# Gathers without GpSimd's rests, and empty list slots read from spread table rows, in a four-layer graph network

## The chip, the cores and the metric

The kernel runs on one core of a Trainium2 chip. The metric is the device time of one execution in microseconds. Engines: PE (matrix), ACT (scalar), DVE (vector), POOL (GpSimd) and SP, which only issues transfers here.

## The reference, cut to what matters

Four graph layers update x (8192 rows of 128 features) with one adjacency matrix of 8192 x 8192 floats, in which about 9 entries of a row are not zero (a density of 0.000976562, and the diagonal). Layers 0, 1 and 3 multiply by the matrix. Layer 2, around which the change lies, takes a maximum over gathered rows:

```python
h = jnp.maximum(_layernorm(x, axis=-1), 0.0)          # layer 2
h = jnp.einsum('ni,oi->no', h, W) + b
_, topk_idx = jax.lax.top_k(adj, 32)
x = x + jnp.max(h[topk_idx], axis=1)
```

A row has some 9 positive entries, so its 32 greatest are these and then the first zero columns. The maximum over the first k zero columns is a prefix maximum, which one table row gives.

## The kernel before

The 64 tiles of 128 rows form 16 groups of 4 tiles. Four stages follow each other.

1. **Adjacency pass.** 256 pieces of 128 x 4 x 512 are loaded; PE turns and multiplies them for layer 0 (L655, L667), ACT copies and marks signs, POOL multiplies by column numbers (L498), DVE takes the 8 greatest keys of each row of each piece (L1473). `pick` (from L1257) makes a group's lists from them: for each tile 3 slots for near neighbours and 6 for far ones, one slot for the prefix row, and for what is left over a pool that the 4 tiles of a group share, of 5, 6, 8 or 12 entries (near) and 12, 14, 17 or 22 (far), by the fullest row of the group. "Near" is 2048 columns, whose part of the table is ready early.
2. **Turned pass.** PE multiplies the stored turned matrix for layer 1 in 8 parts (L751). From each part DVE and ACT make 1024 rows of layer 2's table `h_table` in DRAM (`l1_rows`, L1039 stores them). Ahead of the table lie 65 rows: 64 prefix maxima and, as row 64, one of -3.0e38 (stored at L1047). During this pass POOL gathers for 15 near groups and DVE reduces them (`near_group`).
3. **Chunks.** Layer 3's product runs in 16 chunks of 4 tiles: PE multiplies the 8 parts of a chunk (L783, into two sets of PSUM banks in turn) and DVE adds each part into GR (`add_sums`, L1841 and L1843). PE may be one part ahead: part m needs the sums of part m-2. DVE's loop of a chunk has 8 turns; turns 0 to 3 hold `add_sums` and then one tile of the far maxima (`far_tile`: L1680 adds the mask to gathered rows, L1684 reduces, L1689 and L1692 join, L1717 adds to X), turn 4 `stage_list` (the lists of the group two ahead), turns 5 and 6 `far_own_rows` (L1667, L1668) for the next chunk. Of a new X tile ACT and DVE make layer 3's input (`l3_tile`), which PE needs at the chunk's start.
4. **The end of layer 3** and the stores.

**The gathers.** One `indirect_dma_start` (L506) reads 128 table rows of 512 bytes, one per partition ("lane"), by a column of indices that DVE staged. A near group is 16 gathers for the slots and 5 to 12 for the pool; a far group is 24 and 12 to 22. POOL issues them in a fixed order, waits for `idx_staged` at the start of each group and, for the far pool, for `far_pool_free`. At every fifth gather of a group, counted from its first (k = 0, 5, 10, ...), `rest` runs a POOL instruction pair that computes nothing that is used: an addition of 128 x 512 bf16 onto itself (L517) and a fill of 128 x 384 bytes (L518), both behind a wait for the rests before. The late group (group 0's near part, gathered into GR) has no rests. There are 212 rests and 980 gathers.

**Lanes without a neighbour.** In a tile's own slots an empty entry gets the index of the row's prefix row, as slot 0 does (`pick`, at its end). In a pool slot an empty entry gets key = lane, so the 128 lanes read rows 64 to 191 of the table, and a mask hides what they read (L1541).

Of the kernel before, what the change touches and what calls it, by code (L numbers as in the profile page):

```python
# [10 lines left out]
PREFIX = 64  # L11
NEAR = 4
# [6 lines left out]
BURST = 5  # L19
# [56 lines left out]
def build(nc, x, adj, alpha, w0, b0, w1, w2, b2, w3, b3, out):  # L76
# [22 lines left out]
    NKEY = 3  # L99
    KROWS = 2  # L100
# [9 lines left out]
    table = nc.dram_tensor("h_table", (HEAD + N, P), fp32).ap()  # L110
    near_table = table[0:HEAD + NEAR * PIECE, :]
    early_table = table[0:HEAD + LATE * SGW, :]
    table_v = table[HEAD:HEAD + N, :].rearrange("(t p) f -> p t f", p=P)
# [5 lines left out]
    with ctx:  # L119
# [65 lines left out]
        idle_end = sb("idle_end", [P, 384], u8)  # L185
        lane = sb("lane", [P, 1])
# [30 lines left out]
        idle = D[:, 70 * P:72 * P].bitcast(bf16)  # L217
# [145 lines left out]
        rested = sem("rested")  # L363
# [104 lines left out]
        def _(pool):  # L468
# [8 lines left out]
            pool.iota(lane[:, :], [[0, 1]], base=0, channel_multiplier=1,  # L477
# [11 lines left out]
            pool.iota(row_base, [[STRIDE, TPG]], base=-PREFIX, channel_multiplier=0,  # L489
# [18 lines left out]
            def rests(first, last):  # L508
                return len([k for k in range(first, last) if k % BURST == 0])

            RESTS_N, RESTS_F = rests(0, OWN_N + NEAR_POOL), rests(0, OWN_F + FAR_POOL)
            NO_REST = None
# [12 lines left out]

            def pool_gathers(ring, rows, index, n, cuts, done, so_far, held):
                def leaf(count):
                    most = ring.shape[1]
                    for k in range(count):
                        if so_far is not NO_REST and (held + k) % BURST == 0:  # L530
                            rest(so_far, held + k)
                        share = most * (k + 1) // count - most * k // count
                        gather(ring[:, k, :], rows, index[:, k:k + 1], done, 16 * share)
                    if so_far is not NO_REST and rests(held + count, held + most):
                        pool.sem_inc(rested, 2 * rests(held + count, held + most))
# [5 lines left out]
                with pool.Else():  # L541
                    pool_gathers(ring, rows, index, n, cuts[1:], done, so_far, held)

            def near_gathers(q, n, staged, so_far):
# [3 lines left out]
                own_gathers(near_own[par], near_table, idx_own[par], near_gathered[par], so_far)  # L548
                pool_gathers(near_pool[par], near_table, idx_pool[par], n, NEAR_CUTS, near_gathered[par],
                             so_far, OWN_N)  # L550

            def far_gathers(g, n, staged, free, so_far):
# [3 lines left out]
                own_gathers(far_own[par], table, idx_own[par], far_own_gathered[par], so_far)  # L556
                pool.wait_ge(far_pool_free, free)
                pool.sem_inc(carrier["pool"], 1)
                pool_gathers(far_pools[par], table, idx_pool[par], n, FAR_CUTS, far_pool_gathered[par],
                             so_far, OWN_F)  # L560
# [5 lines left out]
            pool.memset(idle, 0).then_inc(rested, 2)  # L566
            with pool.Fori(0, (NG - 2) // 2) as i:
                for k in range(2):
                    n = pool.value_load(CTL[0:1, 0, bass.ds(i * 2 + (k + 1), 1)], min_val=1, max_val=NEAR_POOL)
                    near_gathers(k, n, i * 2 + (k + 1), i * (4 * RESTS_N) + 2 * k * RESTS_N)  # L570
            n = pool.value_load(CTL[0:1, 0, NG - 1:NG], min_val=1, max_val=NEAR_POOL)
            near_gathers(NG - 2, n, NG - 1, 2 * (NG - 2) * RESTS_N)
            NEAR_RESTS = 2 * (NG - 1) * RESTS_N

            for s in range(SGG, LATE):
# [3 lines left out]
            own_gathers(early_own, early_table, idx_own[1], early_own_gathered, NEAR_RESTS)  # L579
            pool.wait_ge(far_pool_free, 1)  # L580
            pool_gathers(early_pool, early_table, idx_pool[1], n, FAR_CUTS, early_pool_gathered,
                         NEAR_RESTS, OWN_F)

# [15 lines left out]
            own_gathers(late_own, table, idx_own[0], late_gathered, NO_REST)  # L599
            pool_gathers(late_pool, table, idx_pool[0], n, NEAR_CUTS, late_gathered, NO_REST, OWN_N)  # L600

            with pool.Fori(0, (NG - 2) // 2) as i:
                for k in range(2):
                    n = pool.value_load(CTL[0:1, 1, bass.ds(i * 2 + (k + 1), 1)], min_val=1, max_val=FAR_POOL)
                    far_gathers(k + 1, n, i * 2 + (NG + k + 2), i * 2 + (k + 2),
                                i * (4 * RESTS_F) + (2 * (k + 1) * RESTS_F + NEAR_RESTS))
            n = pool.value_load(CTL[0:1, 1, NG - 1:NG], min_val=1, max_val=FAR_POOL)
            far_gathers(NG - 1, n, 2 * NG, NG, 2 * (NG - 1) * RESTS_F + NEAR_RESTS)

        @block.tensor  # L610
        def _(pe):
            pe.wait_ge(s_load, LOADS)
            pe.wait_ge(ident_ready, 4)
# [241 lines left out]
        def _(act):  # L855
# [150 lines left out]
            def l1_rows(s):  # L1006
# [33 lines left out]
                if first == 0:  # L1040
# [6 lines left out]
                    nc.scalar.dma_start(table[0:HEAD, :], pfxn[:, :]).then_inc(head_stored, 16)  # L1047
# [131 lines left out]
        def _(dve):  # L1179
# [78 lines left out]
            def pick(g):  # L1258
# [6 lines left out]
                kn = keys[:, near, :, :].rearrange("p c r e -> p (c r e)")  # L1265
                kfar = keys[:, far, :, :].rearrange("p c r e -> p (c r e)")
# [817 lines left out]
```

## Time and profile before

| what | value |
|---|---|
| device time, median of 3 runs (lowest, highest) | 3695.63 us (3692.3, 3698.97) |
| span of the profiled execution | 3738.5 us |
| PE busy | 3378.0 us, 90% |
| DVE busy | 2622.0 us, 70% |
| POOL busy | 2592.6 us, 69% |
| ACT busy | 1607.0 us, 43% |
| gathers to slots in D, to pool slots in D, to pool slots in ATS | 624 of 1007 ns, 215 of 983 ns, 117 of 1002 ns |
| rests: additions, fills | 212 of 1051 ns, 212 of 428 ns |

The profiled execution has no time of its own beside its span; what lies around the span is not shown. The span is 42.9 us above the median of the runs. Busy time is that of an engine's own instructions; an engine that waits, branches or issues counts as idle. A share of the span is a mean over the four stages.

### The profile page before, as it was taken

Reading aid. Unit: us, or ns where it says so; the run is one execution under the profiler, and the core shown is the slowest. Engines: PE = TensorE matmul, PEld = TensorE weight load, DVE = VectorE, ACT = ScalarE, POOL = GpSimd, SP = SyncE. Lnnn points to the kernel's source line nnn. Section 1 sums busy time; section 2 is a strip of 40 time slices with the busy share of each in tenths; the row PEclk is TensorE's granted clock in tenths of the full one; section 3 lists DMA queues with packets and bytes.
Section 4 is the critical chain, followed back from the end, with each engine's and each line's share of the span. In section 5 each row is a group of like instructions: output and inputs, shape, how many; then the busy total and the mean of one; then the engine's idle time right before and its main releaser. Section 6 shows DMA issues by size and latency. Waiting matters only on the chain.

```text
span 3738.5 us, 76487 instructions
## 1 busy us (share of the span) xinstructions
PE 3378.0 (90%) x29444; PEld 3342.4 (89%) x29444; DVE 2622.0 (70%) x5491; ACT 1607.0 (43%) x3554; POOL 2592.6 (69%) x2448
## 2 busy tenths in 40 slices
PE   6999999999999999999999999942899898989894
PEld 6999999999999999999999999942888898989894
DVE  6788888788788788211177664647787878878767
ACT  6777887787787786222122211221111111112114
POOL 3998998998998997000487856647888878777500
PEclk9999999999999999999999999975999999999997
DMA  6999999999999999788888888842788887878781
GB/s 217 397 396 367 388 385 352 386 389 352 386 391 351 384 376 388 276 291 296 290 322 319 299 294 311 293 154 77 269 286 291 300 308 284 295 280 308 259 293 57
DMA packets 401324, 1155.22 MB, mean 309 GB/s; under 512 B 36717, under 2 KB 56110, under 8 KB 401006
## 3 DMA queue, kind: packets, MB, share of 16 engines
q1 hardware_dynamic: 360096, 1082.21, 78.4%
q0 software_dynamic: 31360, 64.29, 5.5%
q10 hardware_dynamic: 9550, 4.69, 0.4%
q8 instruction: 174, 2.85, 0.3%
q14 instruction: 144, 1.18, 0.1%
HBM read 874.19 MB, written 276.86 MB: 308 GB/s over the span
## 4 chain that ended last, share of the span: by engine, by line
PE 65%; DVE 21%; issue 5%; POOL 4%; ACT 2%; DMA 1%; another core or an unknown queue 1%; DVEq 1%; POOLq 0%; SPq 0%; ACTq 0%
PE psU L667 18%; PE psT L751 18%; PE psT L655 9%; PE psT L783 8%; PE psU L751 6%; DVE agg L1684 4%; DVE HT L1680 3%; PE psU L783 3%; DVE D L1473 2%; POOL D L498 2%; POOL D L506 2%; DVE GR L1843 1%; DVE W L1684 1%; DMA adj_turned<-ATS 1%
## 5 line engine op out<-in xcount | busy, mean ns | idle before, releaser
L498 POOL TENSOR_TENSOR D<-D,iota 128x512 f32<-128x512 f32 x1024 | 1307.3, 1307 | 115.9 <-ACT D L910 97.6
L667 PE MATMUL psU<-HB,ATS 128*128 128x129 f32 x8192 | 1007.1, 276 | 28.4 <-ACT ATS L903 26.3
L667 PEld LDWEIGHTS psU<-HB,ATS 128*128 128x128 f32 x8192 | 961.1, 193 | 33.3 <-ACT ATS L903 28.6
L783 PE MATMUL psT<-ATS,PIECES 128*128 128x129 f32 x6144 | 804.7, 281 | 172.7 <-ACT ATS L1069 79.3
L783 PEld LDWEIGHTS psT<-ATS,PIECES 128*128 128x128 f32 x6144 | 751.5, 196 | 186.3 <-issue 143.8
L1473 DVE MAX8 D<-D 128x8 f32<-128x512 f32 x1024 | 644.2, 683 | 259.7 <-POOL D L498 251.9
L751 PE MATMUL psT<-GR,PIECES 128*128 128x129 f32 x6144 | 780.7, 276 | 20.1 <-issue 19.3
L751 PEld LDWEIGHTS psT<-GR,PIECES 128*128 128x128 f32 x6144 | 733.2, 192 | 24.9 <-issue 24.2
L506 POOL DMA_INDIRECT D<-h_table,idx_own x624 | 628.4, 1007 | 170.4 <-issue 150.3
L903 ACT ACTIVATE ATS<-psT 128x512 f32<-128x512 f32 x1024 | 555.9, 596 | 270.4 <-PE psT L655 177.1
L910 ACT ACTIVATE D<-PIECES 128x1024 f32<-128x1024 f32 x512 | 544.1, 1063 | 0.0
L655 PE MATMUL psT<-ident,PIECES 128*128 128x128 f32 x4096 | 530.7, 273 | 0.0
L655 PEld LDWEIGHTS psT<-ident,PIECES 128*128 128x128 f32 x4096 | 465.1, 142 | 0.1
L751 PE MATMUL psU<-GR,PIECES 128*128 128x129 f32 x2048 | 317.3, 276 | 11.3 <-issue 11.2
L783 PE MATMUL psU<-ATS,PIECES 128*128 128x129 f32 x2048 | 320.3, 279 | 3.2 <-issue 3.0
L517 POOL TENSOR_TENSOR D<-D 128x512 bf16<-128x512 bf16 x212 | 222.8, 1051 | 117.4 <-DVEq L60 103.2
L751 PEld LDWEIGHTS psU<-GR,PIECES 128*128 128x128 f32 x2048 | 272.0, 192 | 14.5 <-issue 14.4
L783 PEld LDWEIGHTS psU<-ATS,PIECES 128*128 128x128 f32 x2048 | 276.4, 196 | 4.9 <-issue 4.8
L1053 ACT ACTIVATE junk_rows<-X 128x128 f32<-128x128 f32 x64 | 19.8, 309 | 569.0 <-DVE X L1717 334.8
L506 POOL DMA_INDIRECT D<-h_table,idx_pool x215 | 211.2, 983 | 71.8 <-issue 53.3
L1843 DVE TENSOR_TENSOR GR<-psT,GR 128x387 f32<-128x387 f32 x240 | 122.5, 552 | 138.0 <-PE psU L783 102.3
L1684 DVE TENSOR_REDUCE agg<-HT 128x128 f32<-128x896 f32 (+2 forms) x120 | 187.4, 1562 | 4.1
(410 smaller groups left out, 2896.9 us busy)
## 6 DMA issues: line engine op xcount, KB each, us to landing
PIECES<-adj_turned SPq DMA_DIRECT2D x512, 1024.0 KB
PIECES<-in_adj SPq DMA_DIRECT2D x256, 1024.0 KB
adj_turned<-ATS SPq DMA_DIRECT2D x512, 512.0 KB, 8.2
D<-h_table,idx_own POOLq DMA_INDIRECT x624
h_table<-HB ACTq DMA_DIRECT2D x8, 512.0 KB, 6.6
D<-h_table,idx_pool POOLq DMA_INDIRECT x215
out_x<-X SPq DMA_DIRECT2D x3, 1024.0 KB, 5.1
ATS<-h_table,idx_pool POOLq DMA_INDIRECT x117
```

Source lines behind the costliest of these rows:

```text
L498: pool.tensor_tensor(key, key, iota[:, :], ALU.mult).then_inc(keyed, 1)
L506: pool.indirect_dma_start(slot, None, rows, bass.IndirectOffsetOnAxis(ap=index, axis=0)).then_inc(done, inc)
L517: pool.tensor_tensor(idle, idle, idle, ALU.add).then_inc(rested, 1)
L655: last = nc.tensor.transpose(psT[h][:, b * GROUP + r * P:b * GROUP + (r + 1) * P], pieces[n % SLOTS][:, r, x0:x0 + P], ident[:, :])
L667: last = nc.tensor.matmul(sum4(r), AT[K % NAT][:, b * GROUP + r * P:b * GROUP + (r + 1) * P], HB[:, j, :], start=(j == 0 and r % 2 == 0), ...
L751: last = nc.tensor.matmul(acc(s % 2, r), block_of(q % SLOTS, b, r), GR[:, j, :], start=(j == 0 and opens(r)), stop=(j == NT - 1 and closes ...
L783: last = nc.tensor.matmul(acc(h, r), block_of(slot, b, r), Hc[par][:, jj, :], start=(jj == 0 and opens(r)), stop=(jj == CT - 1 and closes(r)))
L903: nc.scalar.activation(AT[K % NAT][:, half], psT[K % 2][:, half], ACT.Copy).then_inc(pair_copied, 1)
L910: nc.scalar.activation(KEY[n % NKEY][:, rows, :], pieces[n % SLOTS][:, rows, :], ACT.Sign)\
L1473: last = v.max(cand[g % 2][:, c, r, :], KEY[n % NKEY][:, r, :])
L1684: v.tensor_reduce(part_max[k], kept[:, 0:size, :].rearrange("p k f -> p f k"), AX.X, ALU.max)\
L1843: last = v.tensor_tensor(sums, acc_rows(m % 2, n), sums, ALU.add)
```

## The change

Three things are changed.

- **Rests.** `rest`, its counter `rested`, its tiles and all 212 calls are gone. Waits for `idx_staged` and `far_pool_free` stay.
- **Empty own slots.** `pick` has two more DVE instructions for each group: where a list of 8 keys has an empty entry, it gets the list's first (greatest) key, so that the lane reads its first neighbour's row once more. A list with no key at all still reads the prefix row.
- **Table head and pools.** The 65 head rows are stored 16 times (1040 rows, 532 KB in place of 33 KB), and each 8 lanes use a copy of their own. An empty pool entry has key = 15 x lane (near) or 47 x lane (far), so that lanes read rows spread over the table. DVE has 18 more small instructions before the adjacency pass, to work out each lane's copy.

```diff
+COPIES = 16
-BURST = 5
...
+    NEAR_STEP, FAR_STEP = 15, 47
...
+    BASE = COPIES * HEAD
+    table = nc.dram_tensor("h_table", (BASE + N, P), fp32).ap()
+    heads_v = table[0:BASE, :].rearrange("(c p) f -> p c f", p=HEAD)
...
-            pool.iota(lane[:, :], [[0, 1]], base=0, channel_multiplier=1,
+            pool.iota(lane[:, 0:1], [[0, 1]], base=0, channel_multiplier=NEAR_STEP,
+                      allow_small_or_imprecise_dtypes=True).then_inc(ident_ready, 1)
+            pool.iota(lane[:, 1:2], [[0, 1]], base=0, channel_multiplier=FAR_STEP,
...
-            def rest(so_far, held):
-                pool.wait_ge(rested, so_far + (2 * rests(0, held) + 2))
-                pool.sem_inc(carrier["pool"], 1)
-                pool.tensor_tensor(idle, idle, idle, ALU.add).then_inc(rested, 1)
-                pool.memset(idle_end[:, :], 0).then_inc(rested, 1)
-
-            def own_gathers(ring, rows, index, done, so_far):
+            def own_gathers(ring, rows, index, done):
                 for k in range(ring.shape[1]):
-                    if so_far is not NO_REST and k % BURST == 0:
-                        rest(so_far, k)
                     gather(ring[:, k, :], rows, index[:, k:k + 1], done, 16)
...
-                        if so_far is not NO_REST and (held + k) % BURST == 0:
-                            rest(so_far, held + k)
...
-                    nc.scalar.dma_start(table[0:HEAD, :], pfxn[:, :]).then_inc(head_stored, 16)
+                    nc.scalar.dma_start(heads_v, pfxn[:, :].unsqueeze(1).to_broadcast([HEAD, COPIES, P])).then_inc(head_stored, 16)
...
+                lists, fills = [a.rearrange("p r (l k) -> p (r l) k", k=8) for a in (top, topd)]
...
+                pk.mark(v.scalar_tensor_tensor(fills, lists, 0.0, lists[:, :, 0:1].to_broadcast([P, 2 * TPG, 8]),
+                                               ALU.is_equal, ALU.mult))
...
+                pk.mark(v.tensor_tensor(lists, lists, fills, ALU.add))
...
-                pk.mark(v.tensor_copy(IDXN[:, ts, 0], sp[:, 3, :]))
+                pk.mark(v.tensor_scalar(IDXN[:, ts, 0], sp[:, 3, :], lane[:, 2:3], None, ALU.add))
...
-                link(v.scalar_tensor_tensor(key, empty, lane[:, 0:1], key, ALU.mult, ALU.add))
+                link(v.scalar_tensor_tensor(key, empty, lane[:, 0:1] if near_list else lane[:, 1:2], key, ALU.mult, ALU.add))
...
+            link(v.memset(lane[:, 2:3], 0.0))
+            for k in range(1, COPIES):
+                link(v.scalar_tensor_tensor(lane[:, 2:3], lane[:, 0:1], float(NEAR_STEP * k * (P // COPIES)) - 0.5,
+                                            lane[:, 2:3], ALU.is_gt, ALU.add))
+            link(v.tensor_scalar(lane[:, 2:3], lane[:, 2:3], float(HEAD), None, ALU.mult))
+            link(v.tensor_scalar(row_base, row_base, lane[:, 2:3], None, ALU.add))
```

POOL's order of instructions in a near group, as it was: the last gather to slots (idx_own), with the rest ahead of it, and the pool's gathers (idx_pool) in the case of 5 entries. Ahead of these rows stand three times a rest and five gathers to slots.

```order
L515 REGISTER_ALU
L517 TENSOR_TENSOR D<-D 128x512
L518 MEMSET idle_end 128x384
L506 DMA D<-h_table,idx_own 128x128
L539 COMPARE_AND_BRANCH
L506 DMA D<-h_table,idx_pool 128x128 x4
L515 REGISTER_ALU
L517 TENSOR_TENSOR D<-D 128x512
L518 MEMSET idle_end 128x384
L506 DMA D<-h_table,idx_pool 128x128
```

The whole near group of 21 gathers, as it is now:

```order
L508 DMA D<-h_table,idx_own 128x128 x16
L523 COMPARE_AND_BRANCH
L508 DMA D<-h_table,idx_pool 128x128 x5
```

The four rests of the slots and the one in the pool are gone, and 21 gathers follow each other; nothing else moved. A far group loses eight to ten rests in the same way.

DVE before the adjacency pass, now:

```order
L1860 TENSOR_SCALAR alph<-alph 128x1
L1862 MEMSET lane 128x1
L1864 SCALAR_TENSOR_TENSOR lane<-lane 128x1 x15
L1866 TENSOR_SCALAR lane<-lane 128x1
L1867 TENSOR_SCALAR D<-D,lane 128x4
L1868 COPY psY<-D 128x64
L1869 COPY psY<-own 128x4
```

Of these rows the 18 instructions on `lane` and `row_base` stand between the one on `alph` and the two copies, which were neighbours.

## Rows read from the trace of the kernel before

**Rows 1.** The page: the span, and busy time of each engine.

```profile
span 3738.5 us, 76487 instructions
...
PE 3378.0 (90%) x29444; PEld 3342.4 (89%) x29444; DVE 2622.0 (70%) x5491; ACT 1607.0 (43%) x3554; POOL 2592.6 (69%) x2448
```

**Rows 2.** Chunks: us, busy us (instructions) by engine, PEclk, DMA share, GB/s.

```profile
3000.00:3300.00 300.00, 277.71 (x2366) 273.52 (x2365) 242.51 (x381) 44.99 (x184) 242.12 (x264) 0.97 0.83 298
```

**Rows 3.** PE's waits, 2700 to 3540: us in total, times, longest.

```profile
PE psT L783 <- DVE GR L1843: 52.1, 24, 5.4
PE psT L783 <- issue: 25.9, 37, 3.0
```

**Rows 4.** DVE's and POOL's waits, 2700 to 3540.

```profile
DVE GR L1843 <- PE psU L783: 68.8, 17, 7.0
...
DVE HT L1680 <- issue: 13.6, 15, 1.7
...
POOL D L517 <- DVEq L60: 28.5, 4, 8.3
```

**Rows 5.** POOL in order of time: start, us, what [idle before].

```profile
2835.12 0.94 POOL L506 DMA_INDIRECT D<-h_table,idx_own  x1 [0.30 <-issue]
2836.37 0.94 POOL L506 DMA_INDIRECT D<-h_table,idx_own  x1 [0.30 <-issue]
2837.32 1.06 POOL L517 TENSOR_TENSOR D<-D 128x512 bf16<-128x512 bf16 x1
...
2838.90 0.98 POOL L506 DMA_INDIRECT D<-h_table,idx_own  x1 [0.17 <-POOL idle_end L518]
```

**Rows 6.** DVE in order of time.

```profile
2822.14 1.75 DVE L1680 TENSOR_TENSOR HT<-D,iota 128x768 f32<-128x768 f32 x1
```

**Rows 7.** DVE's groups with rests, 2597 to 3523: busy us, mean ns.

```profile
L1680 DVE TENSOR_TENSOR HT<-D,iota 128x768 f32<-128x768 f32 x32 | 36.2, 1131 | 1.9 <-DVE GR L1849 0.9
...
L1680 DVE TENSOR_TENSOR HT<-ATS,iota 128x768 f32<-128x768 f32 x24 | 28.7, 1194 | 2.7 <-issue 1.3 <-DVE GR L1849 0.9
...
L1689 DVE TENSOR_TENSOR agg<-agg 128x128 f32<-128x128 f32 x55 | 22.3, 405 | 1.9
```

**Rows 8.** The same after the last rest, 3524 to 3600.

```profile
L1680 DVE TENSOR_TENSOR HT<-ATS,iota 128x768 f32<-128x768 f32 x8 | 7.6, 955 | 1.0 <-DVE GR L1849 0.9
...
L1689 DVE TENSOR_TENSOR agg<-agg 128x128 f32<-128x128 f32 x5 | 1.5, 292 | 0.2
```

**Rows 9.** DVE at the start of the chunks, in order of time.

```profile
2579.90 1.61 DVE L1623 TENSOR_TENSOR HB<-HB,agg 128x128 f32<-128x128 f32 x1
...
2620.89 1.09 DVE L1680 TENSOR_TENSOR HT<-ATS,iota 128x896 f32<-128x896 f32 x1 [10.48 <-issue]
```

**Rows 10.** PE at the start of the chunks, in order of time.

```profile
2630.25 2.95 PE L783 MATMUL psT<-ATS,PIECES 128*128 128x129 f32 x12 [8.33 <-DVE GR L1841]
...
2697.90 2.47 PE L783 MATMUL psT<-ATS,PIECES 128*128 128x129 f32 x12 [3.82 <-issue]
```

**Rows 11.** PE's waits in the turned pass with gathers, 1820 to 2460.

```profile
PE psT L751 <- issue: 18.2, 30, 1.1
PE psU L751 <- issue: 11.2, 21, 1.0
```

**Rows 12.** Stretches around two rests (columns of Rows 2).

```profile
2011.50:2013.00 1.50, 1.50 (x16) 1.50 (x15) 0.00 (x0) 1.37 (x8) 1.44 (x3) 1.00 1.01 407
...
2042.80:2044.30 1.50, 0.91 (x9) 0.89 (x9) 1.47 (x2) 0.00 (x0) 1.41 (x3) 1.00 0.87 333
```

**Rows 13.** Queues, 2700 to 3540: packets, MB, share of 16 engines.

```profile
q1 hardware_dynamic: 54316, 209.43, 68.4%
q0 software_dynamic: 16049, 32.89, 12.3%
```

**Rows 14.** DVE waiting in the adjacency pass: in total, and the first time.

```profile
DVE D L1473 <- POOL D L498: 251.9, 202, 3.9
...
63.36 1.29 DVE L1473 MAX8 D<-D 128x8 f32<-128x512 f32 x2 [3.87 <-POOL D L498]
```

More of the change, by code:

```diff
@@ L506, in gather, with pool_gathers @@
                 pool.indirect_dma_start(slot, None, rows, bass.IndirectOffsetOnAxis(ap=index, axis=0)).then_inc(done, inc)
[L508 to L512, printed above, removed]
-            def rest(so_far, held):
-                pool.wait_ge(rested, so_far + (2 * rests(0, held) + 2))
-                pool.sem_inc(carrier["pool"], 1)
-                pool.tensor_tensor(idle, idle, idle, ALU.add).then_inc(rested, 1)
-                pool.memset(idle_end[:, :], 0).then_inc(rested, 1)
-            def own_gathers(ring, rows, index, done, so_far):
+            def own_gathers(ring, rows, index, done):
                 for k in range(ring.shape[1]):
-                    if so_far is not NO_REST and k % BURST == 0:
-                        rest(so_far, k)
                     gather(ring[:, k, :], rows, index[:, k:k + 1], done, 16)
-            def pool_gathers(ring, rows, index, n, cuts, done, so_far, held):
+            def pool_gathers(ring, rows, index, n, cuts, done):
                 def leaf(count):
@@ L541, in pool_gathers, with near_gathers @@
                 with pool.Else():
-                    pool_gathers(ring, rows, index, n, cuts[1:], done, so_far, held)
-            def near_gathers(q, n, staged, so_far):
+                    pool_gathers(ring, rows, index, n, cuts[1:], done)
+            def near_gathers(q, n, staged):
                 par = q % 2
@@ L598, in _ @@
             pool.wait_ge(idx_staged, NG + 1)
[L599 to L600 removed]
+            own_gathers(late_own, table, idx_own[0], late_gathered)
+            pool_gathers(late_pool, table, idx_pool[0], n, NEAR_CUTS, late_gathered)
             with pool.Fori(0, (NG - 2) // 2) as i:
@@ L1353, in pick @@
                 for into, (_, to, count) in zip((IDXN[:, ts, 1:], IDXF[:, ts, :]), parts):
-                    pk.mark(v.tensor_tensor(into, topd[:, :, to:to + count],
-                                            sp[:, 3, :].unsqueeze(2).to_broadcast([P, TPG, count]), ALU.add))
+                    pk.mark(v.scalar_tensor_tensor(into, topd[:, :, to:to + count], lane[:, 2:3],
+                                                   sp[:, 3, :].unsqueeze(2).to_broadcast([P, TPG, count]),
+                                                   ALU.add, ALU.add))
                 pk.settle()
@@ L1544, in stage_list @@
                 link(v.scalar_tensor_tensor(at_row, o3, -float(STRIDE), at_row, ALU.mult, ALU.add))
-                mark(v.tensor_scalar(idx_pool[par][:, 0:count], at_row, float(PREFIX), None, ALU.add))
+                mark(v.tensor_scalar(idx_pool[par][:, 0:count], at_row, float(BASE - 1), None, ALU.add))
                 mark(v.tensor_scalar(keep[par][:, 0, 0:count], keep[par][:, 0, 0:count], NOT_HERE, None, ALU.mult))
```

50 lines of the change are left out of this document (19 added, 31 removed).

## The prediction

> **What bounds the kernel now.** I read the page first: the span is 3738.5 us and PE is busy for 90% of it [rows 1]. A share is a mean over stages, so I then read the waits of PE in each stage that has gathers; the adjacency pass has none, and nothing there waits for them. In the turned pass PE waits for no other engine to speak of: from 1820 to 2460 it stands still 18.2 + 11.2 = 29.4 us in 51 short pauses of 1.1 us at most that the trace gives no releaser for [rows 11]. PE is the bound of that stage, so these pauses count in full. In the chunks PE works 277.7 of 300 us, DVE 242.5 and POOL 242.1 [rows 2], and POOL's figure leaves out 0.30 us of issue behind each gather [rows 5], so POOL hardly rests there either. Who waits for whom tells more: PE waits 52.1 us for DVE's sums and 25.9 us more without a releaser [rows 3], pauses up to 3.0 us long that fall on the same turns; DVE waits 68.8 us for PE but only 13.6 us, 15 times, before the first mask addition of a group; POOL waits 28.5 us for DVE [rows 4]. So the bound of the chunks is PE, held up in turns 0 to 3 by DVE's far tiles, and not the gathers. Only at the stage's start is it the gathers: DVE stands 10.48 us before the first far tile [rows 9], and PE then 8.33 us and, a chunk later, 3.82 us [rows 10].
>
> **The rests, POOL's own time.** Two gathers start 1.25 us apart, and 2.53 us with a rest between them [rows 5]: a rest takes 1.28 us of POOL. 212 of them are 271 us, nearly all where nobody waits for POOL. The exception is the start. Group 1 has 8 rests, 8 x 1.28 = 10.2 us, before its last gather, and DVE's wait is 10.48 us [rows 9]: it goes almost whole. Of PE's 8.33 + 3.82 = 12.2 us behind it [rows 10] I take **12 us**. What is late next is DVE itself, which had finished its other work 10.5 us before; from then on POOL's start on a group is set by DVE's `stage_list`, so the rest of POOL's time turns into longer waits for DVE.
>
> **The rests, DVE's stalls.** A mask addition of 128 x 768 takes up to 1.75 us where a rest runs beside it [rows 6], and 955 ns after the last rest [rows 8]. Over the chunks the mean with rests is 1131 ns of 32 and 1194 ns of 24 [rows 7]: (1131 - 955) x 32 + (1194 - 955) x 24 = 5.6 + 5.7 = 11.4 us for this one shape. L1689 stalls by (405 - 292) x 55 = 6.2 us [rows 7, 8]. The shape 128 x 896 (56 of them) I take at half a stall of these, 0.12 us each: 7 us. With some 9 us for the others (L1692, L1717, L1849, other widths), an estimate at the same share, about 33 us of stall fall in turns 0 to 3. Where DVE sets the pace of these turns PE gets this back one for one, where PE does, nothing: bounds 0 and 33, and since two thirds of the groups have lists of 14 entries or more and show PE waiting, I take **23 us**. Before the chunks' start a stalled L1623 takes 1.61 us [rows 9] and 292 ns unstalled by the nearest like instruction [rows 8]; four of them are on the path to the first chunk, **4 us**. The clock: PEclk is 0.97 from 3000 to 3300 [rows 2]; PE waits stand ahead of what is lost. Of some 900 us the missing 3% is 27 us, and for the waits that go I take a fifth of it, **5 us**.
>
> **The rests, PE's pauses.** Rows 12 show a rest after five gathers and one after two: 1.5 us hold 9 matmuls in the one and 16 in the other. A rest alone therefore costs PE nothing; five gathers and a rest do. The pauses are 29.4 us in the turned pass [rows 11] and in the chunks I take half of the 25.9 us [rows 3], 12 us, since the longer ones of up to 3.0 us look like waits for DVE. What ends when the rests go is open: all 41 us (the rest is needed for a pause), nothing, or it gets worse (below). The span is also 42.9 us longer than the median run, close to this sum, so the recorded execution may have pauses that others lack. I take a third, **14 us**, and keep 0 and 41 as ends. [...]
>
> **The spread rows.** The gathers' queue moved 32.89 MB for 12.3% of the DMA engines, the loads' 209.43 MB for 68.4% [rows 13]: 0.374 against 0.327 % per MB. If spreading made gathered rows as cheap as loads, 32.89 x 0.047 = 1.6% of DMA time would be free; if it cost as much more, the 80.7% in use would be 82.3%. PE waits for no load that a row shows, so either way I count 0. DVE's two instructions for each group (32 in all, under 0.5 us each by the small groups' durations: at most 16 us) lie in the adjacency pass, where DVE waits 251.9 us for POOL [rows 14]; its 18 instructions before that pass, at about 0.2 us each 3.6 us, fit in the 3.87 us for which it waits first [rows 14]. The larger head store (0.5 MB once, ACT's queue) is half a store of a table part, eight of which are hidden. All 0; if the cover were gone, 4 us.
>
> **The sum.** 12 + 23 + 4 + 5 = 44 us, and 14 us of pauses: 58. The profiled span would be 3738.5 - 44 - 41 = 3654 us if all pauses went. The median run: 3695.6 - 58 = 3638, rounded to **3640 us**.
>
> **Rivals.**
> - *The burst, slower.* PE's pause begins with the backlog of some four gathers and the rest only ends it. For it: after two gathers there is none [rows 12], and the 5 may mark where it begins. Against: most of a pause lies within the rest itself. Then, with no rest, PE would go on at 9 in place of 16 matmuls per 1.5 us, 44% lost, until POOL stands still. If each of 15 near groups lost 44% of 12 us and each of 15 far groups 44% of 20 us, that is 79 + 132 = 211 us, less the 44: 3695.6 + 167 = 3863 us. It decides from about 3 us of such slow work per group (44 / 0.44 / 30). Milder forms lie between 3700 and 3770.
> - *PE has it anyway.* The denser gathers (one per 1.25 us, 52 KB/us in place of 43) hold up loads, whose engines are in use for 83% [rows 2], and DVE's time saved is lost to waits for PE (68.8 us now, rows 4). Then only the start's 16 us remain: 3680 us.
> - *The change does not do what it says.* If many lanes on one row were no cost (0.374 against 0.327 allows it), the spread is without effect and the rests decide alone: the forecast stands, or the first rival. It has no chance of its own.
> - *All pauses go, in every run*: 3695.6 - 44 - 41 = 3611 us.
>
> **How the numbers follow.** Forecast 0.44; all pauses go 0.14; PE has it anyway 0.15, of which a third within 0.2%; the burst 0.27, of which 0.02 ends within 0.2%. A measurement of this kernel tells about 0.2% (7 us) from no change. Faster: 0.44 + 0.14 + 0.10 = 0.68. Same: 0.05 + 0.02 = 0.07. Slower: 0.25. The range takes in the forecast with its bounds, 3611 less 16 for stalls that all count, and of the burst what is milder than 3770: 3595 to 3770 us. About 0.17 lies above it, next to nothing below.
>
> **What would show it.** POOL's gathers 1.25 us apart through a group; mask additions of 128 x 768 near 955 ns throughout; no 10 us wait of DVE at the start of the chunks; PE's waits for L1843's counterpart down by a third; longer idle times of POOL. Wrong: PE with more and longer pauses inside groups of gathers than 51 and 1.1 us in the turned pass, or PE waiting for loads.

## The result: 26% slower, and the profile after

The change takes 4658.0 us (median of 4 runs, 4654.2 to 4662.1), the kernel before on the same chip 3697.3 us. The ratio is 1.2609, 95% interval 1.2592 to 1.2627. Forecast were 3640 us and a range up to 3770; the sign belongs to the first rival, which gave 3863 us. In the profiled execution the span is 4652.5 us where it was 3738.5 [rows 1], 914 us more. By the timed runs it is 961 us: the trace of the kernel before is 41 us longer than its timed runs on this chip, and as long as those on three other chips below (3737 to 3742 us). One run of the first experiment below took 5209.99 us at a granted clock of 0.629; it stays unexplained and is left out of that experiment's ratio.

The page of the change: the span, busy time, and the slices of PE, of its granted clock and of the DMA engines (tenths, 40 slices).

```profile
span 4652.5 us, 75668 instructions
...
PE 3568.3 (77%) x29444; PEld 3479.4 (75%) x29444; DVE 2532.9 (54%) x5541; ACT 1609.7 (35%) x3554; POOL 2247.9 (48%) x2024
...
PE   6999999999999998576685781366666565666695
...
PEclk9999999999999999787897885677777777777897
DMA  6999999999999887465675662355555554555673
```

PE has the same 29444 matmuls and is busy for 190 us more: its clock is granted at 0.861 of full speed on average, where it was 0.963, and a matmul that stands alone shows as 0.38 us where in a full row one is done every 0.11 us (65 in 7.00 us, below). The other 724 us are idle time of PE. No other engine is loaded more: DVE and POOL fell [rows 1], the DMA engines moved 248 GB/s over the span where it was 309, and ACT is where it was. The stretches say where (us, busy us and instructions of PE, PEld, DVE, ACT, POOL, then PEclk, DMA share, GB/s):

```profile
0.00:1480.00 1480.00, 1415.73 (x12562) 1408.21 (x12563) 1191.11 (x2632) 1141.95 (x1963) 1304.49 (x1037) 0.99 0.97 367
1480.00:1800.00 320.00, 318.90 (x2854) 318.55 (x2853) 84.40 (x330) 85.06 (x292) 8.08 (x8) 1.00 0.84 294
1800.00:2300.00 500.00, 344.24 (x2684) 332.06 (x2682) 178.80 (x451) 71.88 (x232) 184.21 (x192) 0.80 0.60 200
...
3300.00:3800.00 500.00, 331.41 (x2527) 316.07 (x2527) 241.31 (x437) 54.02 (x220) 161.03 (x171) 0.79 0.56 188
```

The adjacency pass and the first part of the turned pass are as before to within 1% of PE's matmuls (12562 and 2854 in the first two stretches, 12651 and 2866 before). The loss starts within 10 us of the first gather, which comes at 1823.8 us. From 1800 to 2300 PE does 2684 matmuls; in the kernel before it did 4158 in the same stretch, with a clock of 1.00. PE's waits from 1500 to 4600 (total, times, longest):

```profile
PE psT L761 <- issue: 429.0, 252, 74.4
PE psT L729 <- issue: 209.5, 164, 3.1
PE psU L761 <- issue: 163.2, 94, 3.8
PE psU L729 <- issue: 73.6, 55, 2.4
PE psT L761 <- DVE GR L1826: 48.8, 24, 4.7
```

875 us in 565 pauses have no releaser by these four rows. One of them, of 74.4 us, is no new loss: it is PE's wait between the layers, which the kernel before has too. First the row of the change, then that of the kernel before:

```profile
2924.13 2.94 PE L761 MATMUL psT<-ATS,PIECES 128*128 128x129 f32 x12 [74.42 <-issue]
```

```profile
2597.80 2.94 PE L783 MATMUL psT<-ATS,PIECES 128*128 128x129 f32 x12 [79.28 <-ACT ATS L1069]
```

That leaves 801 us, where the two stretches of [rows 3, 11] had 25.9 and 29.4 us. The wait for DVE's sums (L1826, before L1843) is what it was. No row has PE waiting for a load from 1500 to 4600, while SP waits with its loads (L439) 797.8 + 472.7 us for matmuls of PE, and 1190.9 us for what the trace does not name, from 1800 to 4600. One run of gathers shows the pattern, the 38 gathers from 3040.9 on (columns as above):

```profile
3041.00:3048.00 7.00, 7.00 (x65) 7.00 (x64) 6.83 (x11) 0.00 (x0) 5.48 (x6) 1.00 0.89 322
3048.00:3088.00 40.00, 9.03 (x36) 6.90 (x35) 1.97 (x3) 0.00 (x0) 30.24 (x33) 0.57 0.29 82
3088.00:3097.00 9.00, 4.58 (x18) 4.14 (x18) 1.36 (x3) 0.00 (x0) 0.08 (x1) 0.50 0.18 46
3097.00:3102.00 5.00, 5.00 (x43) 5.00 (x42) 0.78 (x2) 0.00 (x0) 0.00 (x0) 0.91 0.92 351
```

For 7 us and 6 gathers PE keeps its 9.3 matmuls per us. Then it does 36 in 40 us, a tenth, until the last gather, and 18 in the 9 us behind it. Then it is back. Seen singly, in another run of gathers (start, us, what [idle before]), first PE and then POOL in the same microseconds:

```profile
1863.36 0.38 PE L729 MATMUL psU<-GR,PIECES 128*128 128x129 f32 x1 [2.42 <-issue]
1866.16 0.38 PE L729 MATMUL psU<-GR,PIECES 128*128 128x129 f32 x1 [2.42 <-issue]
...
1890.66 0.38 PE L729 MATMUL psT<-GR,PIECES 128*128 128x129 f32 x1 [0.32 <-issue]
1891.36 0.38 PE L729 MATMUL psT<-GR,PIECES 128*128 128x129 f32 x1 [0.32 <-issue]
```

```profile
1862.92 0.95 POOL L508 DMA_INDIRECT D<-h_table,idx_own  x1 [0.30 <-issue]
1864.18 0.94 POOL L508 DMA_INDIRECT D<-h_table,idx_own  x1 [0.31 <-issue]
```

One matmul comes every 2.8 us in the middle of a piece, where no semaphore is waited for, and after the last gather one every 0.70 us. PE's granted clock is 1.00 up to 3048 us, and is 0.57 and then 0.50 in the stretches behind it: 1.00 still from 3050 to 3052, when PE already pauses (2 matmuls in 2 us), 0.88 from 3052 to 3054 and 0.50 from there. I call this state of PE **starved**, without saying of what. Of the parts that I had expected, one is plain to see: DVE's mask additions (L1663, before L1680) are at their undisturbed 955 ns of [rows 8], from 3000 on:

```profile
L1663 DVE TENSOR_TENSOR HT<-D,iota 128x768 f32<-128x768 f32 x32 | 30.6, 957 | 1.9 <-DVE GR L1832 0.9
```

### The profile page after: what moved, and what is told of

Same layout as the page of the kernel before. It is cut to its first block, busy times and chain, and to the rows that moved or that the text cites. A ratio compares the mean times of both kernels' runs of the same rounds, so it can differ in the third digit from the quotient of the medians.

```text
span 4652.5 us, 75668 instructions
## 1 busy us (share of the span) xinstructions
PE 3568.3 (77%) x29444; PEld 3479.4 (75%) x29444; DVE 2532.9 (54%) x5541; ACT 1609.7 (35%) x3554; POOL 2247.9 (48%) x2024
## 3 DMA queue, kind: packets, MB, share of 16 engines
q0 software_dynamic: 31360, 64.29, 5.2%
## 4 chain that ended last, share of the span: by engine, by line
PE 63%; issue 19%; DVE 15%; ACT 1%; DMA 1%; DVEq 1%; POOL 0%; SPq 0%; ACTq 0%
PE psU L645 17%; PE psT L729 16%; PE psT L761 11%; PE psT L633 8%; PE psU L729 5%; PE psU L761 4%; DVE agg L1667 3%; DVE HT L1663 2%; DVE GR L1826 1%; DVE D L1456 1%; DVE W L1667 1%; POOL D L500 0%; DVE agg L1672 0%; DMA adj_turned<-ATS 0%; DVE X L1980 0%
## 5 line engine op out<-in xcount | busy, mean ns | idle before, releaser
L508 POOL DMA_INDIRECT D<-h_table,idx_own x624 | 595.2, 954 | 1650.2 <-DVEq L60 1218.0
L761 PE MATMUL psT<-ATS,PIECES 128*128 128x129 f32 x6144 | 888.5, 289 | 481.3 <-issue 429.0
L761 PEld LDWEIGHTS psT<-ATS,PIECES 128*128 128x128 f32 x6144 | 809.3, 204 | 529.1 <-issue 518.5
L729 PE MATMUL psT<-GR,PIECES 128*128 128x129 f32 x6144 | 835.5, 283 | 211.5 <-issue 210.6
L729 PEld LDWEIGHTS psT<-GR,PIECES 128*128 128x128 f32 x6144 | 774.4, 199 | 232.7 <-issue 232.6
L1826 DVE TENSOR_TENSOR GR<-psT,GR 128x387 f32<-128x387 f32 x240 | 122.6, 552 | 681.8 <-remote 553.4
L761 PE MATMUL psU<-ATS,PIECES 128*128 128x129 f32 x2048 | 346.5, 288 | 163.6 <-issue 163.2
L761 PEld LDWEIGHTS psU<-ATS,PIECES 128*128 128x128 f32 x2048 | 294.8, 203 | 167.5 <-issue 167.5
L729 PE MATMUL psU<-GR,PIECES 128*128 128x129 f32 x2048 | 333.0, 283 | 73.7 <-issue 73.6
L729 PEld LDWEIGHTS psU<-GR,PIECES 128*128 128x128 f32 x2048 | 285.6, 199 | 78.2 <-issue 78.2
L1791 DVE TENSOR_TENSOR HB<-psY,bias 128x512 f32<-128x512 f32 x16 | 11.1, 692 | 498.2 <-PE psY L698 498.2
```

Source lines behind the costliest of these rows:

```text
L508: pool.indirect_dma_start(slot, None, rows, bass.IndirectOffsetOnAxis(ap=index, axis=0)).then_inc(done, inc)
L729: last = nc.tensor.matmul(acc(s % 2, r), block_of(q % SLOTS, b, r), GR[:, j, :], start=(j == 0 and opens(r)), stop=(j == NT - 1 and closes ...
L761: last = nc.tensor.matmul(acc(h, r), block_of(slot, b, r), Hc[par][:, jj, :], start=(jj == 0 and opens(r)), stop=(jj == CT - 1 and closes(r)))
L1826: last = v.tensor_tensor(sums, acc_rows(m % 2, n), sums, ALU.add)
```

## Experiments

Eighteen experiments ran on five chips, called A to E in order of time, with runs of the kernel before beside them: 3737.1 us on chip A, 3737.9 on B, 3670.0 on C, 3671.2 on D and 3742.2 on E. These chips turned out to matter, so each result is told with its chip. No chip was used at two times, so what is said of a chip may also belong to its hour. All are edits of the kernel before, unless it is said that they start from the change.

### Chip A: rests or spread rows

The change with `BURST`, `rest` and its two instructions put back, word for word:

> The change with the rests put back: spread rows, and an addition and a fill before every fifth gather as before. Theory A (the missing rests alone make PE slow: it issues one matmul per 2.8 us while gathers follow each other, and the rests ended such spells): back to 3697 us, within 15 us. Theory B (the spread rows do it: lanes without a neighbour read 16 heads and many more places of the table, and that traffic holds up what PE's queue is fed by): it stays above 4300 us, since the rests cover only one gather in five. A mixture would lie between.

Measured: 3745.1 us, ratio 1.0026 (1.0006 to 1.0045). The expected 3697 us was the time of the kernel before on the result's chip; against the 3737.1 us of this one the loss is gone. Its pauses in the turned pass, 1820 to 2460, are those of before and fewer:

```profile
PE psT L757 <- issue: 17.0, 33, 1.0
PE psU L757 <- issue: 6.7, 14, 0.8
```

The counterpart takes only the rests away (`at_rest` also stands in the two conditions ahead of `rest`):

```diff
-            def rests(first, last):
-                return len([k for k in range(first, last) if k % BURST == 0])
+            def at_rest(k):
+                return False
+
+            def rests(first, last):
+                return len([k for k in range(first, last) if at_rest(k)])
```

> The kernel before with nothing taken away but the rests; lanes without a neighbour still read one row. Theory A: as slow as the change, 4658 us within 20. Theory B: no slower than 3700. If the spread had been a help beside the loss (many lanes on one row slow a gather by 50 ns), this one is slower than the change, by up to 30 us.

Measured: 4672.2 us, ratio 1.2508 (1.2471 to 1.2545). Theory A holds from both sides: the missing rests are the whole loss, and the spread rows have no part in it beyond 0.3%. Then the rest in pieces:

```diff
             def rest(so_far, held):
...
-                pool.tensor_tensor(idle, idle, idle, ALU.add).then_inc(rested, 1)
-                pool.memset(idle_end[:, :], 0).then_inc(rested, 1)
+                pool.memset(idle_end[:, :], 0).then_inc(rested, 2)
```

> The kernel before with the rest's addition left out and its fill of 384 bytes kept (some 0.3 us in place of 1.28). Theory A1 (PE recovers as soon as GpSimd does any instruction of its own between gathers): PE stays as before and DVE's stalls beside the additions go, 33 us of them in turns 0 to 3: 3650 to 3680 us. Theory A2 (PE recovers by the length of the pause in the gathers, about 1.3 us per five): the pause is a quarter, and most of the loss of 961 us comes back: above 4200 us.

The next one fills `idle_end[:, 0:8]` in its place:

> As the run with the fill alone, but a fill of 8 bytes per lane, as short as an instruction gets. Theory A1: same as with the full fill, 3650 to 3680 us. Theory A2: as without rests, above 4500 us.

Measured: 4657.8 us, ratio 1.2469 (1.2432 to 1.2505), and 4685.3 us, ratio 1.2536 (1.2499 to 1.2573). It takes more than an instruction between the gathers; A1 is out.

### Chip B: kind of work, length, distance

The addition alone (`.then_inc(rested, 2)`, no fill):

> The kernel before with the rest's fill left out and its addition kept, a pause of some 1.1 us where the whole rest makes 1.28. The two runs with a fill alone (pauses of 0.3 us and less) were as slow as no rest. Theory L (the length of the pause in the gathers counts): about as before, within 60 us, a little slower for the shorter pause. Theory K (the kind of work counts, reading SBUF or adding): the same. If only the two together help, neither holds and it is near 4650 us.

The addition replaced by a fill of the same length (`pool.memset(D[:, 70 * P:72 * P].bitcast(u8), 0)`), with the short fill kept:

> The rest's addition is replaced by a fill of 1024 bytes per lane, about 0.95 us by the rows of shorter fills (120 ns for 8 bytes, 428 ns for 384), so that the pause keeps its length but GpSimd only writes. Theory L: PE as before, and DVE is not held by additions: 3660 to 3745 us. Theory K: as slow as without rests, above 4600 us.

Measured: addition alone 4169.7 us, ratio 1.1188 (1.1124 to 1.1251); two fills 3881.0 us, ratio 1.0383 (1.0364 to 1.0402). Two fills do more than the addition alone and nearly what the whole rest does, so it isn't the kind of work. My bounds of 60 us for the one and of 3745 us for the other were missed: a pause shorter by 0.1 to 0.4 us in five gathers costs 143 to 432 us on this chip. The kernel before stands close to an edge.

The fill of 384 bytes alone, with `BURST = 1`:

> A fill of 384 bytes before every gather in place of a long rest before every fifth: gathers then start 1.55 us apart instead of 1.25 and five of them pause as long in all as five with one rest. Theory R (what counts is how many gathers start in a stretch of time, the mean rate): near the kernel before, 3660 to 3800 us. Theory G (it takes one gap of over a microsecond for PE to recover): above 4400 us.

Measured: **3714.7 us, ratio 0.9937 (0.9916 to 0.9958)**, 0.6% faster than before. POOL in order of time:

```profile
2002.34 0.43 POOL L517 MEMSET idle_end<- 128x384 uint8 x1
2002.93 0.95 POOL L506 DMA_INDIRECT D<-h_table,idx_own  x1 [0.17 <-POOL idle_end L517]
2003.89 0.43 POOL L517 MEMSET idle_end<- 128x384 uint8 x1
2004.48 0.95 POOL L506 DMA_INDIRECT D<-h_table,idx_own  x1 [0.17 <-POOL idle_end L517]
```

Gathers start 1.55 us apart, and PE has no pause without a releaser in the turned pass at all. In place of them come waits of PE for DVE and of DVE for late gathers (2600 to 3540; the second row is DVE's):

```profile
PE psT L782 <- DVE GR L1842: 96.1, 26, 18.7
```

```profile
DVE HT L1679 <- DMA D<-h_table,idx_pool: 67.9, 5, 22.2
```

Whole rests with `BURST = 10`:

> The whole rest, but before every tenth gather. In the kernel before PE loses nothing for the first four gathers behind a rest and about 0.5 us around the next rest. If PE runs at a fifth of its pace from the fifth gather on until a rest, each run of ten loses 5 x 1.25 x 0.8 = 5 us where five lost 0.5: some 90 runs, 3737 + 90 x 4.5 = 4140 us, between 3950 and 4350. If a rest cannot end a spell once it is deep, above 4500 us. If spells begin only after ten or more gathers, below 3800 us.

Measured: 4563.9 us, ratio 1.2202 (1.2176 to 1.2229). That is the third case, a rest can't end a spell once it is deep, and not the 4140 us of the first: a rest is 1.6 us without a gather, and in the change PE takes 5 us and more to come back.

### Chip C: bytes, lanes, pace

```diff
-                pool.indirect_dma_start(slot, None, rows, bass.IndirectOffsetOnAxis(ap=index, axis=0)).then_inc(done, inc)
+                pool.indirect_dma_start(slot[:, 0:16], None, rows.rearrange('n (a f) -> (n a) f', f=16),
+                                        bass.IndirectOffsetOnAxis(ap=index, axis=0)).then_inc(done, inc)
```

> The kernel before without rests, and each gather brings 16 features of 64 bytes per lane in place of 128 features of 512 bytes: 960 gathers of 128 rows each as before, an eighth of their bytes, and the wrong part of the table (it leaves out seven eighths of the gathered features). Theory D (the number of gathers or their descriptors in a stretch of time starves PE): as without rests, 4672 us within 60. Theory Y (their bytes do): below 3800 us.

And, with full rows, `slot[0:64, :]` and `index[0:64, :]`:

> The kernel before without rests, and each gather reads rows for lanes 0 to 63 only (the other lanes' neighbours are left out): the same number of gathers, half the rows and half the bytes. If it is rows per time and a gather of half the rows still starts every 1.25 us, PE is cured: below 3800 us. If such a gather takes GpSimd half as long, rows per time stay what they were, and it depends on the gathers' own pitch. If only the number of gathers counts and the pitch stays at 1.25 us: as without rests, 4672 us.

Measured: 3616.9 us, ratio 0.9843 (0.9815 to 0.9872), and 3619.7 us, ratio 0.9851 (0.9823 to 0.9879), both without one pause of PE in the turned pass, with gathers 1.25 and 1.21 us apart. The gathers' queue (packets, MB, share) moved an eighth and half of the change's 64.29 MB:

```profile
q0 software_dynamic: 31360, 8.09, 1.9%
```

```profile
q0 software_dynamic: 31360, 32.18, 3.1%
```

By the text of the expectations this is theory Y, that bytes matter. It doesn't stand: full gathers without rests weren't run on this chip, and chip D shows that such a chip forgives what the others don't. Bytes or chip, these two runs can't say.

The fill of 256 bytes before every gather:

> A fill of 256 bytes before every gather in place of 384: gathers start about 1.45 us apart, evenly. By the mean distances of gathers in the runs so far (1.25: +935 us; 1.31: +920; 1.38: +826; 1.43: +432; 1.49: +143; 1.51: 0; 1.55: -23) the rate theory says +250 to +450 us, so 3990 to 4190. If an even pace is better for PE than five gathers and a pause of the same mean, less: down to 3720. If the fill before every gather helps by something other than the rate (it waits for the gather's end, say), 3700 us or below, as gathers then come sooner for DVE.

The change's spread rows with the fill of 384 before every gather:

> The change's spread rows with a fill of 384 bytes before every gather. The spread alone measured +0.26%, with an interval from +0.06 to +0.45%, beside whole rests. Theory: the spread is worth nothing once PE is not starved, so this one stands to the kernel before as the run with the fill alone did, 0.9937, within 0.004 (3700 to 3730 us on a chip where the kernel before takes 3737). If the spread has a use, it is below 0.990.

Measured: 3658.3 us, ratio 0.9960 (0.9945 to 0.9975), and 3720.3 us, ratio 1.0124 (1.0101 to 1.0148). The rate theory had wanted 3990 us or more of the first, and falls for this chip; its time lies in the third case, with waits of DVE for gathers (below 3700 us), but chip D shows that this says little of the fill. The second was expected at 0.9937 of the kernel before. Its own time is near what the same pace gave without the spread on chip B (3720.3 against 3714.7); it is the kernel before that takes 68 us less here. Ratios of different chips can't be set against each other where the kernel before is near its edge.

### Chip D: one chip for pace, mean distance and spread

Fills of 128 and of 192 bytes before every gather, the addition alone before every fifth once more, and the spread rows with the fill of 192:

> A fill of 128 bytes before every gather: gathers start about 1.33 us apart, evenly. If an even pace is what PE needs: near 3630 us, as gathers are on time for DVE and no pause is left (thin gathers gave 3617). If there is a rate limit between 1.33 and 1.44 us: 4000 us and more.

> A fill of 192 bytes before every gather: 1.38 us apart, evenly. Mean-rate theory: between the run with rests every tenth gather (mean 1.38, +22%) and the one with additions only (mean 1.43, +11.9%): above 4200 us. Even-pace theory: 3635 to 3655 us, a little below the fill of 256.

> The run with the addition alone, repeated on the chip of the evenly paced ones. Mean distance 1.43 us, but four gathers at 1.25 us between pauses. Even-pace theory: again about +12% on this chip, so slower than the fill of 192 whose mean distance is shorter. If the two chips explained the difference: within 2% of the kernel before.

> The change's spread rows with a fill of 192 bytes before every gather. Spread without effect: within 0.3% of the fill of 192 without it. Spread of use (cheaper rows in DRAM, so shorter gathers or a wider margin before PE starves): more than 0.3% faster, or this one is well where the other is starved. Spread harmful: more than 0.3% slower.

Measured, in this order: **3623.0 us, ratio 0.9878 (0.9860 to 0.9895)**; 3640.5 us, 0.9917 (0.9900 to 0.9933); 3677.0 us, 1.0011 (0.9998 to 1.0024); 3645.4 us, 0.9935 (0.9919 to 0.9952). The mean-rate theory falls for this chip, but the even-pace theory isn't shown either: the addition alone, 11.9% slower on chip B, is as fast as the kernel before here and has no pause without a releaser from 1820 to 2460. The same program behaves otherwise on another chip. Its mask additions, for one, still stall beside the additions of POOL, and those beside fills don't (addition alone, and fill of 128):

```profile
L1679 DVE TENSOR_TENSOR HT<-ATS,iota 128x768 f32<-128x768 f32 x32 | 35.6, 1113 | 3.8 <-DVE GR L1848 1.8 <-issue 1.3
```

```profile
L1679 DVE TENSOR_TENSOR HT<-ATS,iota 128x768 f32<-128x768 f32 x32 | 30.7, 961 | 3.8 <-DVE GR L1848 1.8 <-issue 1.3
```

The spread costs 5.0 us on one chip (3645.4 - 3640.5), within the 0.3% that the expectation calls without effect, but the runs of the two kernels don't overlap, and the trace has its place. DVE before the adjacency pass with the spread rows:

```profile
59.83 8.05 DVE L1891 SCALAR_TENSOR_TENSOR lane<-lane 128x1 f32<-128x1 f32 x15
...
68.10 1.01 DVE L1894 TENSOR_SCALAR D<-D,lane 128x4 f32<-128x4 f32 x1
```

Ten of the fifteen end before POOL's first 128x512 product starts at 61.62 and take 0.16 us each; the last five, beside these products, take 1.15 to 1.21 us. PE in the stretch behind it (us, busy us and matmuls, PEclk, DMA share, GB/s), without and with the spread:

```profile
60.00:200.00 140.00, 139.82 (x1261) 1.00 0.98 380
```

```profile
60.00:200.00 140.00, 134.72 (x1198) 0.99 0.95 361
```

### Chip E: the best and the change on one chip

> The fill of 128 bytes before every gather, repeated. On a chip where the kernel before takes near 3671 us: 0.988 of it again. On one where it takes 3697 or 3737 us: if an even pace of 1.33 us is what keeps PE fed, 0.97 to 0.98 of it (3620 to 3640 us); if the limit of such a chip is the mean rate, near 1.5 us per gather, it is starved like the fill before every fifth gather (mean 1.31 us, +25%): above 4300 us.

> The change itself, repeated on the same chip as the evenly paced kernel. If its loss belongs to the kernel, +24% or more on any chip. If it belongs to the chip: on a chip where the kernel before takes near 3671 us it is not starved and comes to what I had forecast, about 3620 to 3640 us; on one with 3697 or 3737 us it is at 4650 us or more again.

Measured: the fill of 128 before every gather 4613.3 us, ratio 1.2315 (1.2288 to 1.2342); the change 4685.9 us, ratio 1.2522 (1.2496 to 1.2548). Both came as their expectations say for a chip on which the kernel before takes 3697 us or more. The fastest full kernel of one chip is 23% slower than before on another. Where PE was fed through a run of gathers on chip D (first fence, 3327 to 3370), it starves here after 7 us (second fence; columns as in [rows 2]):

```profile
3320.00:3327.00 7.00, 7.00 (x65) 7.00 (x64) 6.25 (x11) 1.98 (x10) 5.42 (x9) 1.00 0.96 328
3327.00:3370.00 43.00, 43.00 (x388) 43.00 (x387) 30.79 (x59) 6.17 (x25) 37.70 (x65) 1.00 0.96 342
```

```profile
3650.00:3657.00 7.00, 7.00 (x65) 7.00 (x64) 4.83 (x7) 0.00 (x0) 5.60 (x10) 1.00 0.88 326
3657.00:3700.00 43.00, 18.16 (x64) 13.21 (x62) 4.78 (x7) 0.00 (x0) 36.29 (x63) 0.56 0.30 97
```

POOL issues at the same pace in both, a gather of 0.95 us and a fill of 0.22 us, 1.34 us from start to start.

Set in order by the mean distance of gathers within a run (worked out from POOL's timelines: five or ten gathers, and what stands between them), the three chips on which the kernel before takes 3737 to 3742 us give one curve (only the distance of 1.25 us ran on two of them, and there they agree):

| distance, us | what | ratio | chip |
|---|---|---|---|
| 1.25 | no rest; the change; tiny fill | 1.251; 1.252; 1.254 | A; E; A |
| 1.31 | a fill every fifth | 1.247 | A |
| 1.34 | fill of 128 each | 1.232 | E |
| 1.38 | rest every tenth | 1.220 | B |
| 1.43 | addition every fifth | 1.119 | B |
| 1.49 | two fills every fifth | 1.038 | B |
| 1.51 | the kernel before | 1 | A, B, E |
| 1.55 | fill of 384 each | 0.994 | B |

On the two chips where it takes 3670 us the same axis reads 0.988 at 1.34, 0.992 at 1.39, 0.996 at 1.44 (even) and 1.001 at 1.43 (addition): there nothing is starved, and an evenly paced gather that comes later only costs.

## Why the prediction was wrong, step by step

- **What bounds the kernel**: right. PE was the bound, DVE's far tiles behind it. But the 29.4 us in 51 short pauses [rows 11], which I read as PE's small change, were the edge of a cliff. The 42.9 us between the span and the timed runs, which I took for a hint that some pauses are only in the trace, may as well be the step from one chip to another (3697.3 against 3737 to 3742 us); the record doesn't tell.
- **The start of the chunks, 12 us**: about a third of it came. Where nothing starves (fill of 128, chip D), DVE still waits at this place, 11.15 us where it was 10.48 [rows 9], and PE's 8.33 + 3.82 us [rows 10] are 7.23 + 0.74:

```profile
2567.53 1.09 DVE L1679 TENSOR_TENSOR HT<-ATS,iota 128x896 f32<-128x896 f32 x1 [11.15 <-DMA ATS<-h_table,idx_pool]
```

```profile
2575.63 2.95 PE L782 MATMUL psT<-ATS,PIECES 128*128 128x129 f32 x12 [7.23 <-DVE GR L1840]
```

With half the lanes, no rest and gathers 1.21 us apart (chip C) DVE waits 4.95 us there. So the wait didn't go "almost whole". In the change itself it is down to 1.09 us, but DVE had just stood 62.20 us before it copied PE's sums (L1824, no engine named), while PE, up to the last gather at 2988.4, did one matmul per 2.8 us.

- **DVE's stalls, 23 us and 4 us**: the stalls went as said, 957 ns in place of 1131 to 1194 [rows 7]. In the change itself the worth of the 23 us can't be read, since PE is late everywhere in the chunks. The 4 us ahead of the chunks were too few: PE's two waits between the layers are 40.69 and 74.42 us in the change, and were 45.66 and 79.28, together 9.8 us less. On chip D they are 41.08 and 74.02 us with fills of 128, 45.80 and 79.17 with additions. That the additions alone lengthen them is not shown: the first is 45.3 us also with the fills of 384 before every gather (chip B), the second 78.8 us also without any rest (`e2_rests_gone`, chip A). The best evidence for the sum is the same chip: additions replaced by short fills, 3671.2 - 3623.0 = 48 us faster, beside the 44 us of my sum without the pauses. The kernel before has no trace on that chip, so whether pauses are in it isn't known; the total agrees with the sum, its parts at the chunks' start (12 and 4 us) were dealt out wrongly.
- **New work of DVE, 0 us**: wrong by 5 us. I priced the 18 instructions on `lane` and `row_base` at 0.2 us each, 3.6 us, within the 3.87 us of cover [rows 14]. Fifteen of them take 8.05 us: 0.16 us each, as priced, until POOL's first 128x512 product starts, and the five beside these products 1.15 to 1.21; one more takes 1.01. The cover was gone, and the 4 us that I gave for that case were nearly right.
- **The spread rows, 0**: right but for these 5 us, by one pair on one chip. With rests they make 1.0026.
- **PE's pauses, 14 us gained: this is the step that failed**, and with it the bound of its bad side. I took "all 41 us, nothing, or it gets worse" and let the first two set the sum. The row that I leaned on for the worse case had 9 matmuls in place of 16 in 1.5 us [rows 12], a loss of 44%; the state behind it has 36 in 40 us, a loss of 90%. I let it last for 12 us per near and 20 us per far group. It lasts from the sixth or so gather to the end of the run and some 5 to 12 us beyond until the pace is full again: in the runs of gathers of the change that begin with PE at full pace, its pace falls below half of full after 5 to 8 gathers (counted from the starts of its matmuls in 3 us).
- **The first rival** had the pattern, pauses that begin after a number of gathers and that a rest keeps short, but not the size; that a backlog is behind it isn't shown. With the measured values a near group of 21 gathers loses 0.9 x 14 x 1.25 + 0.8 x 7 = 21 us, and a far one of 38 in a row 0.9 x 31 x 1.25 + 0.8 x 8 = 41 us; 15 of each, an estimate, are 930 us, less the 44: 886 us, where 961 were measured. That is worked out afterwards, from the result's own rows. Its words "the 5 may mark where it begins" were the point: rests after every five gathers stand just under an onset at 5 to 8. A number like that in a kernel is worth asking what it holds off, and the trace of before can't show it, because it never runs six gathers in a row while PE has work: its late group of 24 without a rest (2524.6 to 2556.4 us) lies wholly in PE's wait of 79.28 us.
- **What the pauses hang on.** Not the rests' own work: PE does 16 matmuls in 1.5 us beside a rest [rows 12], and with every rest gone its pauses without a releaser are 801 us. They hang on the gathers: they begin after 5 to 8 of them, and PE is back at its full pace 5 to 12 us behind the last. That they could be in the recorded execution alone, as the 42.9 us made me think, isn't decided by the runs: the four timed runs of the change (4654 to 4662 us) agree with the profiled span of 4652.5 us, but each of them has a span and a granted clock of its own on record, so none is known to have run unrecorded. What they show is that the pauses are not in one profiled execution alone.
- **PE waits for loads**: no. The DMA engines are in use for 29% while PE starves (3048 to 3088), and no load is among the releasers of PE's waits; of SP's waits from 3000 to 3100, 41.8 us are for PE and 50.4 us have no engine named.

What stays open: what PE lacks. The trace gives no releaser. A gather to a tile's own slots takes GpSimd 954 ns on average in the change, 1007 before. A DMA packet of the gathers takes 0.108 us in the starved run with the fill of 128 (chip E) and 0.105 in the fed one (chip D), worked out over the whole run from the queue's share of the 16 engines' span (4.6% of 4612.9 us and 5.7% of 3619.9 us, for 31360 packets). No packet of an instruction queue falls between 3048 and 3088. Whether PE was short of instructions, or held up by the recording, wasn't tested. Whether fewer bytes or lanes per gather feed PE wasn't settled. Why chips differ isn't shown, nor whether the change itself would starve on a chip where the kernel before takes 3670 us; no run had the two together. And what cures on the starving chips is told by mean distance alone: an even pace at 1.34 us didn't help there, but even and uneven weren't compared at one distance between 1.4 and 1.5.

No version is known for both kinds of chip. The fill of 384 bytes before every gather is 0.6% faster on a starving one (0.9937, chip B). On the other kind only its sibling with spread rows ran, 1.2% slower than the kernel before. None was shown to beat both kernels everywhere; the fill of 128 is 1.2% faster or 23% slower, by the chip.

## What to carry to other kernels

Before you take away a pause, ask what its period holds off, and price the state behind the edge by a run and not by the first dip that the trace shows: the dip was 44%, the state 90%, and it lasted for as long as its cause. If PE pauses in the middle of a piece with "issue" as the only reason while GpSimd gathers without a break, space the gathers (here 1.55 us from start to start in place of 1.25) before you look for anything else. And time such an edit on more than one chip: near this edge the kernel before differs by 2% from chip to chip, and an edit by 24 points.

## What the runs showed of the hardware

- Back-to-back indirect gathers of 128 rows of 512 bytes by GpSimd (1.25 us apart) bring PE down to one matmul per 2.8 us after 5 to 8 of them, and keep it below its pace for 5 to 12 us after the last; PE's granted clock is then 0.50 to 0.57. It happened on the result's chip and on A, B and E (on B with the spacings up to 1.49 us). On these the turn between nearly all and nothing lies between 1.38 us (ratio 1.220) and 1.51 us (1) per gather.
- On chips C and D PE has no pause without a releaser from 1820 to 2460 at 1.44 us (fill of 256, ratio 0.996) and 1.34 us (fill of 128, 0.988). The kernel before takes 3670 and 3671 us there, in place of 3697 to 3742.
- Beside fills by GpSimd of 128 to 384 bytes per lane before every gather (0.22 to 0.43 us each; chips D and B) DVE's mask additions of 128x768 take 955 to 967 ns on average, as in the change without any (955 and 957); beside additions of 128x512 bf16 before every fifth gather they take 1092 and 1113 ns (chip D).
- DVE's operation on one element per lane took 0.16 us before POOL's first 128x512 product and 1.15 to 1.21 us beside these products (10 and 5 of them, spread rows with the fill of 192).
